# Both ends of the expert stage re-ordered in a two-layer vision transformer kernel

## What is computed

```python
scores = sigmoid(x @ gate_w.T)                       # (T, 32)
choice = scores + gate_bias                          # 4 groups of 8, the 2 best groups kept, then the 8 best
topk_w = 2.5 * w / w.sum()                           # w: scores of the 8 chosen
out_e  = (silu(x @ Wg[e].T) * (x @ Wu[e].T)) @ Wd[e].T
h      = h + sum_e topk_w[t, e] * out_e + shared(x)  # shared: an ungated expert of inner width 256
```

## Time and profile before

| | |
|---|---|
| Median of 3 runs | 417.8 us (417.43 to 422.83) |
| Profiled execution | 418.78 us, its span 417.0 us |
| TensorE busy | 386.8 us (93%), 3269 matmuls |
| VectorE, ScalarE, GpSimd busy | 258.8, 187.5, 131.3 us (62, 45, 31%) |
| Granted TensorE clock, mean | 0.98 of full speed |
| DMA | 32.96 MB |

### The profile page before, as it was taken

The page is one execution under the profiler, slowest core; times in us unless marked ns, Lnnn a source line. Parts: engine busy times, 40 slices in busy tenths (PEclk is TensorE's granted clock), DMA queues, the critical chain, the costliest instruction groups (busy, mean ns, idle before and its releaser), DMA issues.

```text
span 417.0 us, 8560 instructions
## 1 busy us (share of the span) xinstructions
PE 386.8 (93%) x3269; PEld 314.5 (75%) x3269; DVE 258.8 (62%) x525; ACT 187.5 (45%) x401; POOL 131.3 (31%) x109
## 2 busy tenths in 40 slices
PE   8898699998999899999999999999988999999675
PEld 6554478656787687999999999999986755567333
DVE  0258877589876854555555555555564558844686
ACT  0154722348342533444444554444435488634171
POOL 0125300163030052344333334433385047620012
PEclk9999989998999999999999999999999999999798
DMA  8940000300042006254554554444200000000001
GB/s 300 331 173 2 3 3 2 101 0 4 2 163 66 0 9 230 68 137 134 135 145 145 155 142 147 134 134 146 84 0 0 2 0 2 2 3 1 0 2 58
DMA packets 13916, 32.96 MB, mean 79 GB/s; under 512 B 1760, under 2 KB 3744, under 8 KB 13376
## 3 DMA queue, kind: packets, MB, share of 16 engines
q1 hardware_dynamic: 12000, 30.66, 23.4%
q10 hardware_dynamic: 1888, 1.91, 1.3%
HBM read 31.88 MB, written 0.68 MB: 78 GB/s over the span
## 4 chain that ended last, share of the span: by engine, by line
PE 69%; DVE 19%; ACT 5%; issue 4%; DMA 2%; ACTq 1%; POOL 0%; DVEq 0%
PE psum L1087 68%; DVE rc L847 3%; DMA region<-in_w_lin 2%; DVE rn L826 1%; ACT region L725 1%; DVE xn L774 1%; DVE nt L768 1%; DVE rn L825 1%; DVE nt L770 1%; DVE nt L771 1%; DVE region L848 1%; DVE xc L759 1%; DVE ra L816 1%; ACT sq L541 1%; DVE al L985 1%
## 5 line engine op out<-in xcount | busy, mean ns | idle before, releaser
L1087 PE MATMUL psum<-xh,split_all 128*128 128x296 f32 x544 | 122.9, 300 | 1.4 <-DVE rt L927 1.3
L443 POOL TENSOR_TENSOR split_all<-km,split_all 128x768 fp32r<-128x768 f32 x34 | 63.3, 1863 | 115.9 <-ACT split_all L654 115.9
L1087 PEld LDWEIGHTS psum<-xh,split_all 128*128 128x128 f32 x544 | 91.7, 188 | 2.7 <-DVE rt L927 1.8
L1087 PE MATMUL psum<-xl,split_all 128*128 128x296 f32 (+1 forms) x288 | 85.1, 300 | 0.0
L1087 PE MATMUL psum<-ah,split_all 128*128 128x296 f32 x272 | 67.6, 302 | 2.6 <-DVE al L985 2.0
L674 ACT ACTIVATE ah<-rt 128x296 fp32r<-128x296 f32 x68 | 30.7, 452 | 80.6 <-DVE rt L983 74.3
L1087 PEld LDWEIGHTS psum<-xl,split_all 128*128 128x128 f32 (+1 forms) x288 | 53.2, 187 | 3.2 <-issue 2.8
L985 DVE TENSOR_TENSOR al<-rt,ah 128x296 fp32r<-128x296 f32 x64 | 31.9, 498 | 33.1 <-ACT ah L674 33.1
L1087 PEld LDWEIGHTS psum<-ah,split_all 128*128 128x128 f32 x272 | 47.8, 189 | 5.0 <-DVE al L985 2.5
L980 DVE TENSOR_TENSOR rb<-psum,wb 128x296 f32<-128x296 f32 x60 | 28.0, 467 | 26.4 <-ACT psum L672 26.4
L1087 PE MATMUL psum<-al,split_all 128*128 128x296 f32 x136 | 40.8, 300 | 0.0
(11 more groups left out here) (179 smaller groups left out, 579.0 us busy)
## 6 DMA issues: line engine op xcount, KB each, us to landing
km<-in_experts SPq DMA_DIRECT2D x34, 384.0 KB, 4.0
wb<-weights SPq DMA_DIRECT2D x30, 296.0 KB, 3.7
w_sb<-in_w SPq DMA_DIRECT2D x2, 1024.0 KB, 11.9
region<-in_x SPq DMA_DIRECT2D x6, 296.0 KB, 5.5
region<-in_g_wo SPq DMA_DIRECT2D x1, 1024.0 KB, 4.9
region<-in_l_wo SPq DMA_DIRECT2D x1, 1024.0 KB, 5.0
region<-in_w_lin ACTq DMA_DIRECT2D x6, 128.0 KB, 6.7
qkv_sb<-in_qkv_w SPq DMA_DIRECT2D x1, 768.0 KB, 6.0
```

The costliest lines, as they stand in the source:

```text
L443: nc.gpsimd.tensor_tensor(wl[i], ring[i], wh[i].bitcast(f32), ALU.subtract)\
L1087: return nc.tensor.matmul(out_, lhsT, rhs, start=start, stop=stop, skip_group_check=True)
```

## The change

Constants and order only; what is computed stays the same.

- Norm: no warming matmuls between mean and variance, the peak rows are put there (bank 6); the peak reduction goes ahead of the normalisation, the scales ahead of the routing chain.
- Splits: all four ring units are split ahead of the norm, on ScalarE and on GpSimd; so SP can load units 4 to 7 before it comes to the routing weights.
- Shared units: half 0 uses banks 4 and 5, half 1 banks 6 and 7, so that the up sums of both halves of unit 0 wait for nothing. The first use of banks 6 and 7 now waits for the sigmoid and the scales.
- `down_sums` issues the four matmuls with the high part `ah` first, then waits for the low part and issues the last two. This holds for every unit.
- Units 2 and 3: `selected_weights` is gone. SP copies rows 0 and 1 of `wrow` straight from SBUF to all partitions of `wb`. The store to memory and the rows of units 4 to 7 follow behind.
- GpSimd's work on the feed-forward weights is cut into 8 pieces for each tensor and the clearing into 8; one piece follows the low part of each unit from unit 4 on.

```diff
-BUSY = (..., (3, (5, 4, 8)), ...)
+BUSY = (..., (3, (5, 0, 8)), ...)
+WPIECES, VPIECES = 8, 8
@@ sync
             for u in range(NRING, 2 * NRING):
-                if u == NRING + 2:
-                    sp.wait_ge(s_wrow, 2)
-                    sp.dma_start(weights, wrow[:, 0:T]).then_inc(s_wout, 16)
-                    sp.wait_ge(s_wout, 16)
-                    for i in range(NRING):
-                        spread_weights(i, weights[NRING + i - SHARED:NRING + i - SHARED + 1, :])
                 load_expert(u, experts[u, :, :])
+            sp.wait_ge(s_wrow, 2)
+            for u in range(SHARED, NRING):
+                sp.dma_start(wb[:, u, :], wrow[u - SHARED:u - SHARED + 1, :].unsqueeze(1).broadcast_to([1, P, T]))\
+                    .then_inc(s_wb[u], 16)
+            sp.dma_start(weights, wrow[:]).then_inc(s_wout, 16)
+            sp.wait_ge(s_wout, 16)
+            for u in range(NRING, 2 * NRING):
+                if u % NRING >= SHARED:
+                    sp.wait_ge(s_act, 2 * (u + 1 - NRING))
+                spread_weights(u % NRING, weights[u - SHARED:u - SHARED + 1, :])
@@ gpsimd
-            low_part(0, 0) ... activation_low_part(3, 1)          # alternating
+            for i in range(NRING):
+                low_part(i, i)
+            for n in range(2 * SHARED):
+                activation_low_part(n, n % 2)
+            def quantise_piece(k):
+                w, wq_ = ((w1_sb, w1q), (w2_sb, w2q))[k // WPIECES]
+                cols = slice(k % WPIECES * WPIECE, (k % WPIECES + 1) * WPIECE)
+                nc.gpsimd.tensor_scalar(w[:, cols], w[:, cols], inv[:, k // WPIECES:k // WPIECES + 1], ROUND,
+                                        ALU.mult, ALU.add).then_inc(s_wqt, 1)
+                pool.wait_ge(s_wqt, k + 1)
+                nc.gpsimd.tensor_scalar(wq_[:].rearrange("p c n -> p (c n)")[:, cols], w[:, cols], 1.0, -ROUND,
+                                        ALU.mult, ALU.add).then_inc(s_wq, 1)
-            # after the last unit: 2 + 2 tensor_scalar of 2048 columns, memset of 4352 columns, ones
+            for u in range(NRING, UNITS):
                 low_part(u, u % NRING)
+                k = u - NRING
+                if k < 2 * WPIECES:
+                    quantise_piece(k)
+                elif k < 2 * WPIECES + VPIECES:
+                    clear_piece(k - 2 * WPIECES)
+                ...
@@ scalar
-            for i in range(AHEAD):
+            for i in range(NRING):
                 high_part(i, i, 0, False)
             norm(2)
+            load_table(ACT.Sigmoid)                               # was behind the copies to xh
...
+            for i in range(SHARED):
+                for j in range(2):
+                    expert_unit(2 * i + j, j, sg[:, j, :], 4 + 2 * j)
+            for i in range(SHARED, NRING):
+                if i == SHARED:
+                    act_e.wait_ge(s_wrow, 2)
+                expert_unit(2 * i, 0, ps[6][:, 0:HALF])
+                high_part(i + AHEAD, (i + AHEAD) % NRING, (i + AHEAD) // NRING)
+                expert_unit(2 * i + 1, 1, ps[7][:, 0:HALF])
@@ vector
             centre(2)
+            reduce_peaks(0, 2, 6, 1)
             norm_apply(2, 6)
...
-            reduce_peaks(0, 2, 7, 1)
+            scales_of(0, 2, 7, 1).then_inc(s_sc, 1)
...
             for u in range(SHARED, NRING):
+                dve.wait_ge(s_wb[u], 16)
                 for j in range(2):
-                    dve.wait_ge(s_sel, 2 * (u - SHARED) + j + 1)
-                    expert_unit(2 * u + j, j, sg[:, j, :], ps[6 + j][:, 0:HALF])
+                    expert_unit(2 * u + j, j, ps[6 + j][:, 0:HALF], wb[:, u, half(j)])
@@ tensor
             def down_sums(u, i, hf, shared=False):
                 n = 2 * u + hf
+                pe.wait_ge(s_ah, n + 1)
+                for m in range(C):
+                    cols = slice(2 * D + m * P, 2 * D + (m + 1) * P)
+                    for w in (wh, wl):
+                        mm(ps[2 * m + hf][:, 0:HALF], w[i][:, cols], ah[:, hf, :], False, False)
                 if shared:
                     pe.wait_ge(s_alp, n + 1)
                 else:
                     pe.wait_ge(s_al, n + (1 - 2 * SHARED))
                 for m in range(C):
-                    ins = three(...)
+                    ins = mm(ps[2 * m + hf][:, 0:HALF], wh[i][:, cols], al[:, hf, :], False, False)
...
-            up_sums(0, 0, 1)
+            pe.wait_ge(s_sig, 1)
+            pe.wait_ge(s_sc, 1)
+            up_sums(0, 0, 1, 6, 0)
             down_sums(0, 0, 0, shared=True)
-            up_sums(1, 1, 0)
+            up_sums(1, 1, 0, 4, 1)
             down_sums(0, 0, 1, shared=True)
-            up_sums(1, 1, 1)
+            up_sums(1, 1, 1, 6, 2)
             down_sums(1, 1, 0, shared=True)
             pe.wait_ge(s_wts, 1)
+            pe.wait_ge(s_act, 2 * SHARED)
             ...                                                   # transposes to banks 6 and 7
-            selected_weights(...)                                 # four calls among units 2 and 3
```

More of the change, by code:

```diff
@@ L32 @@
 TT = 5
+LAST = T - (TT - 1) * P
 FF = 1024
@@ L450, in activation_low_part @@
                     .then_inc(s_alp, 1)
[L452 to L463, removed]
-                low_part(u, u % NRING)
@@ L467, in _ @@
[L467 to L474, removed]
@@ new lines, in clear_piece @@
+            def clear_piece(k):
+                cols = slice(k * VPIECE, (k + 1) * VPIECE)
+                nc.gpsimd.memset(region[:, cols], 0.0).then_inc(s_vz, 1)
+            for u in range(NRING, UNITS):
+                low_part(u, u % NRING)
+                k = u - NRING
+                if k == 0:
+                    pool.wait_ge(s_sc, 1)
+                    pool.wait_ge(s_wo, 4)
+                if k < 2 * WPIECES:
+                    quantise_piece(k)
+                elif k < 2 * WPIECES + VPIECES:
+                    clear_piece(k - 2 * WPIECES)
+                elif k == 2 * WPIECES + VPIECES:
+                    pool.wait_ge(s_vz, 1 + VPIECES)
+                    pool.wait_ge(s_wsl, u + 1)
+                    for b in range(2):
+                        nc.gpsimd.memset(v16[64 * b:64 * b + S, :, :, b, HD:HD + 1], 1.0).then_inc(s_vz, 1)
+                    pool.wait_ge(s_vz, VZ)
@@ L667, in _, with expert_unit @@
             load_table(ACT.Silu)
-            def expert_unit(n, j, gate):
+            def expert_unit(n, j, gate, bank=4):
                 act_e.wait_ge(s_g, n + 1)
-                nc.scalar.activation(gate, ps[4][:, 0:HALF], ACT.Silu).then_inc(s_sg, 1)
+                nc.scalar.activation(gate, ps[bank][:, 0:HALF], ACT.Silu).then_inc(s_sg, 1)
                 act_e.wait_ge(s_act, n + 1)
                 nc.scalar.activation(ah[:, j, :], act[:, j, :], ACT.Copy).then_inc(s_ah, 1)
[L676 to L679, removed]
+            for i in range(SHARED):
[7 more added lines that the diff above has]
+                expert_unit(2 * i + 1, 1, ps[7][:, 0:HALF])
             with act_e.Fori(1, (UNITS - AHEAD) // NRING) as r:
@@ L1369, in three, with up_sums @@
                 return mm(out_, w_lo, x_hi, False, stop)
-            def up_sums(u, i, hf, first=False):
-                n = 2 * u + hf
+            def up_sums(u, i, hf, bank=4, waits=None):
+                n = 2 * u + hf if waits is None else waits
                 if hf == 0:
                     pe.wait_ge(s_wsl, u + 1)
-                if not first:
+                if waits != 0:
                     pe.wait_ge(s_sg, n)
@@ L1379, in up_sums @@
                     cols = slice(c * INNER, (c + 1) * INNER)
-                    ins = three(ps[4][:, 0:HALF], (wh[i][:, cols], wl[i][:, cols]),
+                    ins = three(ps[bank][:, 0:HALF], (wh[i][:, cols], wl[i][:, cols]),
                                 (xh[:, c, half(hf)], xl[:, c, half(hf)]), c == 0, c == C - 1)
                 ins.then_inc(s_g, 1)
-                if not first:
+                if waits != 0:
                     pe.wait_ge(s_act, n)
@@ L1408, in down_sums @@
                     cols = slice(2 * D + m * P, 2 * D + (m + 1) * P)
[L1409 to L1410 removed]
+                    ins = mm(ps[2 * m + hf][:, 0:HALF], wh[i][:, cols], al[:, hf, :], False, False)
                 ins.then_inc(s_down, 1)
             pe.wait_ge(s_xs, 1)
[L1415 removed]
+            up_sums(0, 0, 0, 4, 0)
             seed(1)
[L1417 removed]
             pe.wait_ge(s_xs, 2)
[L1419 removed]
+            pe.wait_ge(s_sig, 1)
+            pe.wait_ge(s_sc, 1)
+            up_sums(0, 0, 1, 6, 0)
             down_sums(0, 0, 0, shared=True)
[L1421 removed]
+            up_sums(1, 1, 0, 4, 1)
             down_sums(0, 0, 1, shared=True)
[L1423 removed]
+            up_sums(1, 1, 1, 6, 2)
             down_sums(1, 1, 0, shared=True)
             pe.wait_ge(s_wts, 1)
[L1427 to L1429 removed]
+            pe.wait_ge(s_act, 2 * SHARED)
+            mm(ps[6][0:EXPERTS, 0:LAST], wts[:, TT - 1, :], const("ident")[:, 0:LAST], True, True)
```

(3 more changed lines are left out.)

51 lines of the change are left out of this document (14 added, 37 removed).

## The result

The changed kernel takes **427.45 us** (median of 4 runs, 426.39 to 428.65) against 417.62 for the kernel before, run beside it (median of 4): ratio 1.0245, 95% interval 1.0202 to 1.0289, so slower, by 9.8 us. One of those four runs (422.83) fell in a slower state and is not in the ratio; without it the medians are 10.0 us apart. Its profiled execution took 426.39 us with a span of 424.6.

What follows compares the result with a forecast made beforehand. The prediction took TensorE, busy throughout the middle of the expert stage, as the bound. Its terms, +12.3 to unit 4's activation, +2.4 clock and -1.8 end, made +12.9 us: 430.7 us against the median, range 426.5 to 437.

Steps and rivals of the forecast that it cites:

- The rows' start: Start of the expert stage: weight rows ready at 153.1, 2.0 us earlier; bounds 155.1 and 152.1.
- The pace of the copy: First two weight rows, each copied from one SBUF partition: 27.1 GB/s, 11.2 us a row.
- The landing: First row copy: packets from 0.9 us after the issue, row read at 165.2, landed at 165.4.
- Unit 2 to unit 3: Second row follows in the same queue: first weighted activations at 166.5 for unit 2 and 177.7 for unit 3.
- Unit 3 to unit 4, with the clock: Unit 4's activation 4.86 us after unit 3's; low clock after TensorE's idling adds 2.4, bounds 0 and 3.2.
- The end: End of the expert stage: -1.3 us from GpSimd pieces, -0.5 from earlier last down sums, together -1.8; bounds -2.3 and 0.
- The loads of experts 4 to 7: SP's queue: it passes its waits for these loads earlier; nothing waits for them, so 0.
- The cover on GpSimd: Loop: a piece costs GpSimd about 0.3 us twice per unit beside one split, hidden on an engine 31% busy.
- Rival (3): Loop: GpSimd's pieces stop VectorE, 24 units times up to 0.3 us, up to 438 us; chance 0.04.
- (1): First routed rows: copy from one partition as fast as one from memory, 3.7 us, total 413.3 us; chance 0.10.
- (2): First routed rows: the SBUF outlet is twice as wide, rows of 5.6 us, total 417.1 us; chance 0.04.
- (4): First routed rows: every partition is its own bottleneck, 41 us a row, total about 490 us; chance 0.02.

Runs made afterwards that it cites:

- e11: e4 with GpSimd's splits of experts 2 and 3 back between the activation low parts: 413.73 us in one run.
- e10: e4 with the down sums in the old order, the low part between the high ones: 414.18 us, ratio 0.9943 to the kernel before.
- e6: Changed kernel with each row copy cut into 8 DMAs of 16 target partitions, issued in turn from SP, reading partitions 0 and 1: 431.53 us.
- e7: As e6, but unit 3's row is read from partition 16 instead of partition 1: 424.05 us.
- e9: e4 with GpSimd's feed-forward quantisation and clearing back behind the loop, in operations of 2048 columns: 413.51 us, ratio 0.9927 to the kernel before.
- e8: Kernel before with only its selecting matmuls replaced by the two row copies from SBUF, plus the waits needed: 438.05 us, ratio 1.0551.
- e1: Changed kernel with the second row (partition 1) copied from ScalarE's queue at the same time as SP issues the first: 432.26 us in one run.
- e4: Changed kernel with the four selecting matmuls of the kernel before in place of the two row copies: 412.42 us, ratio 0.991 to the kernel before.
- e3: Changed kernel without the two SBUF copies, rows of units 2 and 3 stored to memory and spread: 414.67 us, ratio 0.9958 to the kernel before.

## Why the prediction was right, step by step

The mechanism and the sign hold: slower through the copy from one partition, at the pace named. The size is 9.8 us by the medians (10.0 without the run of 422.83) where I had 12.9 against the profiled execution. By the steps:

- **The rows' start** (-2.0): -1.96. The sum is right, its parts less so. The order on GpSimd makes 1.1 of it (e11), where I had 0.7 and 0.3 for the two blocked VectorE operations. The low parts placed last make 0.55 (e10); I had no such term, only "a few tenths" for another edit. That leaves 0.3 for the earlier sigmoid and the moved scales, which I put at 0.75. That the sum came out is in part luck.
- **The pace of the copy** (27.1 GB/s, 11.2 us a row): in the trace's DMA packets the first one starts at 152.62 and the last of the two rows ends at about 175.0, so 11.2 us a row and 27.1 GB/s. The cause shows in e6 and e7: 26 GB/s with partitions 0 and 1, 52 with 0 and 16.
- **The landing** (0.9 us to the first packet, 0.2 behind the last): 1.2 and 0.3 to 0.4. Rows to unit 2 was to take 13.4 us and took 14.45: 0.3 by the later first packet and 0.8 in the first row itself, whose DMA engines finish their shares between 162.9 and 164.5. That the early ones go on with the second row meanwhile is my inference, from both rows together keeping the pace.
- **Unit 2 to unit 3** (11.2): 10.6. The second row gets back what the first lost.
- **Unit 3 to unit 4, with the clock** (4.86 + 2.4 = 7.26): **this is the term that was mis-sized.** First weighted activations end at 176.46 and 182.07, so 5.61. No run shows the 2.4 that I put in for the clock. The trace of the changed kernel has the clock at 0.50 over 176.5 to 178, 0.66 over 179 to 180 and 1.00 from 180 on, so low for some 3.2 us of work, as it was for 3.4 us in the 0.57 over 52 to 56; by my estimate from the 5.61 it cost about 1.6, within my bounds. What I left out: while TensorE waited for the second row it had done the gate sum of the next half already, 6 matmuls of 0.135 = 0.81 us. 4.86 - 0.81 + 1.6 = 5.65. It is also one reason why TensorE stood 3.88 us there and not the 6 that I gave as a sign of being right.
- **The end** (-1.8): -2.68. The stall near 309 makes -1.4 and the last down sums -0.5, as said. The remaining 0.8 are the pace of the loop, 737 matmuls in 100 us before and 742 after, for which I had no term and which no run here ties to the change. In e9 the pieces alone are worth 0.81, since with high parts first a blocked low part is half hidden: the two edits overlap, and my 1.3 and 0.5 were right as a sum but not as two separate values.
- **The loads of experts 4 to 7** (0): nothing waited for them in the kernel before, but behind slow copies on the same queue two of them cost a third stall (e8). The term was 0 only because the change moved them too.
- **The cover on GpSimd**: a piece of 256 columns takes 0.78 us and one with bf16 output 0.41, not 0.3 each; GpSimd's busy time grows from 131.3 to 141.5 us, and nothing waits for it. Both and a split of 1.84 in one unit are 3.0 of 4.9 us. Rival (3) did not come about: low parts 469 ns.
- Rivals (1), (2) and (4) fall with e6 and e7: 26 to 28 GB/s for the rows of partitions 0 and 1 together, 52 for those of 0 and 16.

The sum of the steps was 12.9 and the stage grew by 10.84: start 0, first row +1.05, second row -0.6, third step -1.65, end -0.9, in all -2.1. The errors have both signs and partly cancel. The remaining 1.0 up to the 9.8 of the medians I can't place: the profiled executions differ by 3.2 us outside the stage, and the median of the kernel before is itself known only to about 1 us (417.6 here, 416.2 to 417.0 beside the experiments). The terms of my range for the lower bound add up to 426.8 and not 426.5, which decides nothing.

## What to carry to other kernels

A row that sits in one partition left SBUF at 26 to 28 GB/s in every form tried here (one DMA or eight, SP's queue or ScalarE's), so to spread it over 128 partitions is 11 us for 296 KB. From the moment the row was ready to the end of the first product with it took 14.4 us with that copy, 6.4 by a detour over memory and 3.5 with a one-hot matmul. Estimate a direct copy by the partitions it reads, not by the landing time of a copy with the same target. Take each consumer the path that just meets its time (a matmul for the first, memory for the next), and judge a compound change by undoing its parts one at a time: here one of them hid a gain of some 4 us. Before a small difference between two traces is put down to an edit, look for it among traces that share the code: the pace of the loop differed by 0.7% between them.

## What the runs showed of the hardware that I had not expected

- Two queues, one copy each with all 16 engines: the copies were served one after the other and not in turn (e1: 92.1% of the engines to q10, then 90.3% to q1). In DMAs of 16 target partitions on one queue they ran side by side (e7: 52 GB/s).
- A packet of the copy out of SBUF (2,368 bytes) took about 1.27 us, with up to 16 under way (after; e1: 93 packets in 8 us at 92.1% of 16 engines). The copies landed 0.3 to 0.4 us behind the end of the last packet (after: 164.5 and 164.80, 175.0 and 175.42). The issue took 0.58 us (after, L375) where that of a row from memory took 0.33 (L369).
- The same loop, with TensorE always busy and the granted clock at 1.00, ran 742 matmuls in 100 us in some executions (after, e4) and 737 in others (before, e3, e7). Why is open.
- A wait of 3.90 us of TensorE lowered the clock as one of 11.90 did (e3: 0.53 over 160 to 165; after: 0.56 over 165 to 170). Behind the two waits of the changed kernel it was low for 3.2 to 3.5 us, behind that of e3 for 5.1 (0.50 over 162 to 164, 0.67 over 164 to 165), so by my estimate from these stretches a late row cost 1.6 to 2.4 us beyond its wait.
- An eighth of a GpSimd operation did not take an eighth of its time: 256 columns took 0.78 us (after, L466), 2048 columns 1.98 to 2.32 (e9, L464).
